# A four-layer vision network on one core: the selective scan is moved in place into two PSUM banks, the rows of C come by DMA, and one bank is shared by the convolutions, heads, tables and offsets

## The reference

```python
# layers 0, 2, 3, on every image
xp = x @ w_in + b_in
h = gelu(batchnorm(depthwise_conv3x3(x)))
offset = (h @ w_off + b_off).reshape(N, H, W, 4, 9, 2)
mask = softmax((h @ w_msk + b_msk).reshape(N, H, W, 4, 9))
y = (bilinear_sample(pad(xp), pixel + tap + offset) * mask).sum(taps) @ w_out + b_out
x = x + gamma1 * layer_norm(y); x = x + gamma2 * layer_norm(gelu(x @ w_fc1 + b_fc1) @ w_fc2 + b_fc2)

# layer 1: 256 inner channels, 16 states, 4 directions k, L = 3136 pixels
xb = silu(depthwise_conv3x3(xx) + conv_b)         # xx, z = split(layer_norm(x) @ in_proj)
dt, B, C = softplus(...), ..., ...                # per direction, from x_proj(xb)
for t in pixels of direction k:
    h = h * exp(dt_t * A) + dt_t * u_t * B_t      # [256 channels, 16 states]
    y_t = (h * C_t).sum(states)
```

## Time and profile before

| | |
|---|---|
| median of three runs | 33311.78 us |
| the profiled execution | 33289.16 us, its span 33287.3 us |
| busy, share of the span | PE 75%, DVE 67%, ACT 36%, POOL 76% |
| granted TensorE clock, mean | 0.82 |
| DMA engines | 56 GB/s, 1,201,869 packets |

### The profile page before, as it was taken

How to read it: one execution, slowest core, us unless ns; L and a number is a source line. 1 busy time by engine, 2 the same in 40 slices (tenths; PEclk the granted TensorE clock), 3 DMA queues, 4 the chain that set the end, 5 groups by cost and what they waited for, 6 DMA issues and landing times.

```text
span 33287.3 us, 293513 instructions
## 1 busy us (share of the span) xinstructions
PE 24914.8 (75%) x101616; PEld 16138.7 (48%) x101616; DVE 22464.4 (67%) x31608; ACT 11949.6 (36%) x20587; POOL 25332.0 (76%) x21604
## 2 busy tenths in 40 slices
PE   6588787878888887888888788787577876555544
PEld 5444454545445554554455445454454545444443
DVE  1289959896988789789968996997149992211211
ACT  1144434444444444444444444443134442010100
POOL 5787868877887787778778787777777877767767
PEclk7698888888888888898889888888688887666666
DMA  2211121212112121211121112111221212222211
GB/s 64 66 52 52 50 64 43 58 48 62 51 50 58 52 57 47 63 51 50 54 58 57 48 53 65 45 55 52 63 69 44 58 49 67 60 62 61 62 55 51
DMA packets 1201869, 1854.06 MB, mean 56 GB/s; under 512 B 391531, under 2 KB 750493, under 8 KB 1200381
## 3 DMA queue, kind: packets, MB, share of 16 engines
q0 software_dynamic: 691200, 1388.65, 15.4%
q1 hardware_dynamic: 509180, 446.64, 4.2%
HBM read 1568.56 MB, written 265.21 MB: 55 GB/s over the span
## 4 chain that ended last, share of the span: by engine, by line
POOL 33%; PE 27%; DVE 23%; issue 14%; ACT 1%; DMA 1%; DVEq 0%; SPq 0%; POOLq 0%; ACTq 0%
POOL d_g L664 33%; DVE l_wk L1197 10%; PE d_p L928 7%; PE l_acc L915 5%; DVE l_wk L1219 4%; DVE l_wk L1187 3%; PE d_pr L1066 2%; PE d_pr L1065 2%; PE d_pr L1077 2%; DVE d_g L1232 2%; PE l_pm L963 2%; PE l_pc L885 1%; PE d_pr L1131 1%; PE l_pm L941 1%; PE l_pc L1041 1%
## 5 line engine op out<-in xcount | busy, mean ns | idle before, releaser
L664 POOL DMA_INDIRECT d_g<-table,d_idx x21600 | 25331.7, 1173 | 7921.9 <-issue 6559.3
L928 PE MATMUL d_p<-d_g,c_ident 128*128 128x128 f32 x43200 | 6879.2, 331 | 4002.6 <-DVE d_g L1232 4001.5
L928 PEld LDWEIGHTS d_p<-d_g,c_ident 128*128 128x128 f32 x43200 | 6639.9, 241 | 4818.7 <-DVE d_g L1232 3783.0
L915 PE MATMUL l_acc<-l_wk,c_ident 128*128 128x448 f32 x14336 | 7276.6, 637 | 0.4 <-DVE l_wk L1219 0.4
L1232 DVE TENSOR_TENSOR d_g<-d_g,d_wt 128x1536 f32<-128x1536 f32 (+1 forms) x1800 | 3151.5, 1751 | 5481.9 <-DMA d_g<-table,d_idx 5480.1
L1197 DVE TENSOR_TENSOR_SCAN l_wk<-l_wk,l_carry 128x448 f32<-128x448 f32 x6144 | 6715.5, 1133 | 0.0
L1187 DVE TENSOR_TENSOR l_wk<-l_wk,l_pb 128x896 f32<-128x896 f32 x3584 | 3864.5, 1078 | 1609.2 <-PE l_pb L885 1603.5
L707 ACT ACTIVATE l_wk<-l_wk,l_a 128x448 f32<-128x448 f32 x7168 | 4361.8, 656 | 16.4 <-DVE l_wk L1261 3.6
L885 PE MATMUL l_pc<-l_spl,c_sel 96*128 96x448 bf16 x3584 | 1402.4, 391 | 3569.2 <-DVE l_wk L1219 3556.7
L915 PEld LDWEIGHTS l_acc<-l_wk,c_ident 128*128 128x128 f32 x14336 | 3135.8, 219 | 1835.5 <-issue 1717.1
L1219 DVE TENSOR_TENSOR l_wk<-l_wk,l_pc 128x896 f32<-128x896 f32 x3584 | 3798.0, 1060 | 9.3 <-PE l_pc L885 8.6
(11 more groups left out here) (169 smaller groups left out, 22973.9 us busy)
## 6 DMA issues: line engine op xcount, KB each, us to landing
d_g<-table,d_idx POOLq DMA_INDIRECT x21600
table<-d_pst SPq DMA_DIRECT2D x600, 256.0 KB, 2.1
hd<-d_hst SPq DMA_DIRECT2D x168, 224.0 KB
d_htc<-hd SPq DMA_DIRECT2D x144, 256.0 KB
d_xin<-mid SPq DMA_DIRECT2D x112, 224.0 KB, 3.0
mid<-d_xo SPq DMA_DIRECT2D x192, 128.0 KB
d_xres<-mid SPq DMA_DIRECT2D x192, 128.0 KB
d_xin<-in_x SPq DMA_DIRECT2D x56, 224.0 KB, 3.0
```

The lines of the kernel that those rows point to most:

```text
L664: e.indirect_dma_start(out=m.g[Q % SLOTS][0:n, j, :], out_offset=None, in_=m.table[k % 2], in_offset=bass.IndirectOffsetOnAxis(ap=m.idx[G ...
L915: ins = e.matmul(m.acc[:, h, 0:448], m.ident[:, :], m.hb[x % 4][:, h, :], start=(n == 0), stop=(n == 15))
L928: ins = e.matmul(m.p0[0:n, t % 2 * 128:t % 2 * 128 + 128], m.ident[0:n, 0:n], m.g[Q % SLOTS][0:n, 4 * p:4 * p + 4, 32 * r:32 * r + 32], st ...
```

## The change

- **Scan.** `hb` is three tiles in place of four and holds only the product with C. The product with B goes to `l_bb`, two PSUM banks (`m.bb`); both scans run in place there, VectorE copies the last column to `carry` itself (not in the last chunk of a direction), and the product with C reads `l_bb` and writes `hb`. A step now runs whole before the next: product with B, two scans, copy, product with C, each but the last waiting for the one before (`hc`, `f_pb`, `sc`).
- **Rows of B and C.** TensorE spreads only B, one step ahead. C's 16 rows of a piece go to DRAM (`cd`) by DMA at head part 1; SyncE then issues for each step one DMA that repeats a row over 128 partitions into one of three tiles `cb` (229 KB each), two steps ahead.
- **Banks.** `l_pc` and `l_pm` are gone. Layer 1's convolution and head share `m.r[1]` with the stages' `ax`, `ac`, `at` and `pr`. The norms and projections between images use the halves `b0`, `b1` of `l_bb`.
- **Order.** An item that fills `m.r[1]` and the one that empties it are now one item of the list, and at most one such item is put in a tick. Convolutions are done in halves of 224 columns, all nine taps in one tick, so the weights are loaded twice as often. `PREP` is one tick shorter (11 ticks in place of 12, if the bank is free). `xin` is one tile in place of two.

The diff, cut to its core:

```diff
@@ vss_ticks
-                out += [(0.5, [("c", i, c, h, part)]) for part in range(4)]
+                out += [(0.8, [("c", i, c, h, part)]) for part in range(2)]
...
-                if j + 2 < 7 and 8 <= q:
-                    tick.append(("c", i, j + 2, (q - 8) // 4, (q - 8) % 4))
+                if j + 2 < 7 and 8 <= q and q % 2 == 1:
+                    tick.append(("c", i, j + 2, (q - 9) // 4, (q - 9) // 2 % 2))
...
-PREP = [0, 2, 1, 0, 1, 1, 1, 1, 1, 1, 1, 1]
+PREP = [0, 2, 0, 0, 1, 1, 1, 1, 1, 1, 1, 1]
@@ Planner.scan_tick
+            self.used = self.used or x[0] == "c" or x[0] == "h" and x[3] in (0, 3, 5)
@@ Planner.stage_tick
-        if self.loads and self.loads[0][1] <= self.fetched + 1 and self.there(*self.loads[0]):
+        if self.loads and self.loads[0][1] <= self.fetched and self.there(*self.loads[0]):
+            self.loads_at = self.tick
...
+        if self.prep and self.prep[0][0][3] == 1:
+            if not self.used and self.tick - self.prep_at >= PREP[1]:
+                for _ in range(3):
+                    self.put(*self.prep.popleft()[0])
+                self.used, self.prep_at = True, self.tick
+        elif self.prep and self.tick - self.prep_at >= self.prep[0][1]:
+            self.put(*self.prep.popleft()[0])
+            self.prep_at = self.tick
+        if self.ahead and not self.used and self.open(self.ahead[0]):
+            use = self.ahead.popleft()
+            for x in use:
+                self.put(*x)
+            self.used = use[0][0] != "al"
...
+        self.used = False
@@ Mem
-        self.wk = [sb(f"l_wk{i}", [128, 2, 448]) for i in range(12)]
+        self.wk = [sb(f"l_wk{i}", [128, 2, 448]) for i in range(11)]
+        self.cb = [sb(f"l_cb{i}", [128, 448]) for i in range(CROWS)]
+        self.bb = ps("l_bb", [128, 2, 512])
+        self.b0, self.b1 = self.bb[:, 0, :], self.bb[:, 1, :]
+        self.cd = [dram(f"cd{i}", (16, 448)) for i in range(2)]
@@ sync_program
+        elif kind == "h" and item[3] == 1:
+            e.wait_ge(s["hd0"], P + 1)
+            if P >= 2:
+                e.wait_ge(s["hc"], 16 * (P - 1))
+            e.dma_start(m.cd[P % 2], m.bcd[16:32, :]).then_inc(s["cdo"], 16)
+        elif kind == "s":
+            for q in (range(CROWS - 1) if sig == -1 else (sig + CROWS - 1,) if sig >= 0 else ()):
...
+                    if S >= CROWS:
+                        e.wait_ge(s["hc"], S - CROWS + 1)
+                    e.dma_start(m.cb[S % CROWS][:, :], m.cd[P % 2][n:n + 1, :].to_broadcast([128, 448])).then_inc(s[f"cb{S % CROWS}"], 16)
@@ scalar_program
-                e.activation(m.carry[:, :, n], m.hb[(S - 1) % 4][:, :, end], ACT.Copy).then_inc(s["ca"], 1)
@@ tensor_program
-            if 0 <= sig < NSTEP:
-                if J.use["C", S]:
-                    e.wait_ge(s["f_pc"], J.use["C", S])
-                spread(S, m.pc, 16).then_inc(s["p_pc"], 1)
...
-                e.wait_ge(s["f_pc"], J.free("C", x))
+                e.wait_ge(s["hc"], x + 1)
...
+            for j in range(9):
+                dy, dx = 4 * part + j // 3, j % 3
+                ins = e.matmul(m.r[1][:, 0:224], m.cdiag[:, 9 * h + j, :],
+                               m.grid[:, h, 8 * c + dy:8 * c + dy + 4, dx:dx + 56], start=(j == 0), stop=(j == 8))
@@ vector_program
-                e.tensor_tensor(m.hb[x % 4][:, :, :], m.dtu[P % 2][:, :, :], bc(m.pb[:, 0:448], 1, 2),
-                                ALU.mult).then_inc(s["f_pb"], 1)
...
+                if S:
+                    e.wait_ge(s["hc"], S)
+                bu = m.bb[:, :, 0:448]
+                e.tensor_tensor(bu, m.dtu[P % 2][:, :, :], bc(m.pb[:, 0:448], 1, 2), ALU.mult).then_inc(s["f_pb"], 1)
+                e.wait_ge(s["dA"], S + 1)
                 e.wait_ge(s["f_pb"], J.free("B", S))
                 for h in range(2):
                     ini = 0.0 if c == (6 if kd >= 2 else 0) else m.carry[:, h, n:n + 1]
-                    ins = e.tensor_tensor_scan(m.hb[S % 4][:, h, way], m.dA[S % 3][:, h, way], m.hb[S % 4][:, h, way], ini,
-                                               ALU.mult, ALU.add)
+                    ins = e.tensor_tensor_scan(bu[:, h, way], m.dA[S % 3][:, h, way], bu[:, h, way], ini, ALU.mult, ALU.add)
                 ins.then_inc(s["sc"], 1)
+                e.wait_ge(s["sc"], S + 1)
+                if c != (0 if kd >= 2 else 6):
+                    end = 0 if kd >= 2 else 447
+                    e.tensor_copy(m.carry[:, :, n], bu[:, :, end])
+                e.wait_ge(s[f"cb{S % CROWS}"], 16 * (S // CROWS + 1))
+                if S >= 3:
+                    e.wait_ge(s["accd"], S - 2)
+                e.tensor_tensor(m.hb[S % 3][:, :, :], bu, bc(m.cb[S % CROWS][:, :], 1, 2), ALU.mult).then_inc(s["hc"], 1)
...
-                e.wait_ge(s["p_pc"], J.full("C", x))
-                e.wait_ge(s["ca"], x + 1)
-                e.tensor_tensor(m.hb[x % 4][:, :, :], m.hb[x % 4][:, :, :], bc(m.pc[:, 0:448], 1, 2),
-                                ALU.mult).then_inc(s["f_pc"], 1)
```

More of the change, by code:

```diff
@@ L239, in run @@
         self.start_ahead(0)
-        self.drain(lambda: not self.ahead and not self.bank)
+        self.drain(lambda: not self.ahead)
         self.start_prep(0, 0)
-        self.drain(lambda: not self.prep and not self.bank)
+        self.drain(lambda: not self.prep)
         self.chain += [(("lg", 0), 0), (("lg2", 0), 1)]
@@ L251, in run @@
                 if t % 4 == 0:
-                    self.drain(lambda: not self.prep and not (self.bank and self.bank[0][0][0] == "pr"))
+                    self.drain(lambda: not self.prep)
                     if g + 1 < len(GROUPS):
@@ L619, in sync_program @@
             q = 7 * i + c
[L620 removed]
+            e.wait_ge(s["f_b1"], J.free("pt", q))
             if i:
@@ L880, in tensor_program @@
     e.wait_ge(s["cst"], 1)
-    def spread(S, bank, row):
-        P, n = divmod(S, 16)
-        return e.matmul(bank[:, 0:448], m.sel[:, row + n:row + n + 1].to_broadcast([96, 128]), m.spl[P % 2][:, :],
-                        start=True, stop=True)
     for item in J.plan:
```

443 lines of the change are left out of this document (198 added, 245 removed).

## The result

The changed kernel takes **34,278 us** (median of 4 runs, 34,229 to 34,290; 33,288 for the kernel before beside it): **2.9% slower**, ratio 1.0294, interval 1.0276 to 1.0312. I had forecast 32,500 us, 2.4% faster. The profiled execution has a span of 34,279 us, against 33,287.

What follows compares the result with a forecast made beforehand. VectorE with its waits for TensorE bounded the scan stretches, GpSimd the rest. Scans 19,555 + 1,190 + 220 + 750 + 300 = 22,015, rest 10,467, together 32,482: forecast 32,500 us, range 31,500 to 33,650.

Steps and rivals of the forecast that it cites:

- POOL is freed: Beside scans, GpSimd's need falls to about 18,630 us, 16.8 us a third; by itself this buys almost nothing.
- VectorE's step: In scan stretches, new dependences cost 860 and 80 us and the carry copy 246: +1,190 us in sum.
- PSUM operands at 0: VectorE's products and scans with PSUM operands cost nothing extra; bounds -215 to +645 us.
- TensorE: In scan stretches, bunched bank fills against about 9 us of room leave waits for B of 750 us, before 1,603.
- The other waits: VectorE's other idle time in the scan stretches, some 350 us before, was put at 300 us.
- my chief rival: TensorE and ScalarE hand over the one shared bank, holding B back 1.5 us a fill: 34,050 us, chance 0.17.
- The pace: Planner's pace falls from 3.14 to 2.92, 85 more thirds beside scans: -1,314 us outside the stretches, +220 us within.
- Small terms: C's row loads free; +25 us between images, +60 for the shared bank without scans, -120 for GpSimd's earlier start.
- The 120 us that I took off: GpSimd enters the two stretches free of scans some 60 us further ahead: -120 us.
- a step that grows by more than 0.4 us: Sign against the forecast: VectorE's scan step, 4.08 us before, lengthens by more than 0.4 us.
- the rival with 34,050: Shared bank's hand-over between TensorE and ScalarE makes waits 2,300 us, not 750; chance 0.17, left outside the range.
- terms 2 and 4: Scan stretches: VectorE's longer step, +1,190 us, and its waits for TensorE's spread of B, 750 us.

Runs made afterwards that it cites:

- run 302: Not a follow-up run: the words say that 302 us of the 1,797 us missed lie in the rest of the run, outside the scan stretches.
- a_sbuf: Changed kernel with B's product and both scans written in an SBUF tile instead of the two PSUM banks: 34,300 us.
- a_order: Changed kernel with VectorE's two waits ahead of a step's first scan in the other order: 34,152 us.
- a_fill: Changed kernel with TensorE's spread of B moved from behind a third's twelve accumulations to behind the first four: 33,886 us.
- a_sep: Changed kernel with B's product and scans in SBUF, and layer 1's convolutions and heads on the bank this frees: 34,294 us.
- a_prep: Changed kernel with VectorE's two operations that empty the bank of offsets moved to the start of the next tick: 34,118 us.
- a_nocb: Changed kernel with C's rows loaded for the first three steps only and reused in every step: 34,299 us.
- a_short: Changed kernel with one tap of nine in all depthwise convolutions, every wait and emptying kept: 33,569 us.

## Why the prediction was wrong, step by step

The trace's 34,279 us less my sum of 32,482 is 1,797 us. The stretches of scans have 1,495 of it, the rest of the run 302.

1. *POOL is freed*: right. The gathers' mean is 1,030 ns (forecast 1,060). That this is worth nothing by itself is right too (a_sbuf).
2. *VectorE's step*: right mechanism, size too small. I had two dependences at 0.12 us, a copy at 0.08, a fifth of a third dependence, 1,190 us in all. Measured are 0.44 us, 1,580 us. One dependence cost 0.185, because its wait is an instruction of its own (a_order). My 20,965 us for VectorE in the stretches had the dependences in it. To compare, its busy time of 20,789 takes the 376 us of gaps in front of the first scans and 160 us of gaps under 0.06 us: 21,325, **+360 us**.
3. *PSUM operands at 0*: right (a_sbuf, 22 us apart).
4. *TensorE*: **this step failed.** I gave it 9 us of room and put the wait for B at 750; it is 1,391: **+641 us**. I counted the room from the moment at which VectorE frees B's bank. But TensorE works in order, and in a tick with a third it can't begin before VectorE's product L1214, the last of a tick. From there it has one step, 4.5 us, for the accumulations and the spread, not 9; moving the spread forward took off 471 us (a_fill). The end of the 3,557 us wait for C did let TensorE come earlier: where VectorE waits for a spread that has a third ahead of it, the accumulations start 3.0 us after the product's end in the kernel before and 0.15 us in the changed one (medians of 578 of 782 and 576 of 754 waits). But it can't come earlier than the product, and I had the passes too cheap: a third's take 4.13 us, 1.39 a tick, where I put 1.0. At 2.9 us, the time at the upper clock, passes and spread would fit into the step; of the 574 waits right behind a third's passes 467, 892 of 1,144 us, follow passes in which the clock was below 0.95. How much of the +641 the clock accounts for stays open. And 275 of the 574, 911 us, are of another kind than the one shown above: TensorE had no idle time ahead of the third, so it was late already. The other waits, which I put at 300 us, are 794 (345 norms, 334 offsets, 115 others): **+494**. The sharing of the bank by layer 1 and the stages, the core of my chief rival, has no part in either (a_sep); the shared tick has 92 us of the offsets' wait (a_prep).
5. *The pace*: right. The planner found 2.948 (forecast 2.92); 1,202 thirds run beside scans (1,212). The ten thirds are 150 us of the **+302** outside.
6. *Small terms*: C's rows free, right (a_nocb). The shared bank outside the scans was put at +60; ahead of the first scan alone it is 152 us, 92 more (a_short takes 115 of the 152 away). The 120 us that I took off for GpSimd's further start into the two free stretches didn't come: these shrank by 1,176 us, 75 thirds at 15.5 are 1,162. Between the other images it is 22 us less where I had 25 more. With the ten thirds this is the 302.

My own list of signs had "a step that grows by more than 0.4 us" as one that would tell against the forecast. The range ended at 33,650, because I let the rival with 34,050 stay outside, and because terms 2 and 4 both came out high and I had added no case in which they do so together.

What stays open: how much the lower clock costs in the wait for B; of this wait 645 us remain without bunched passes and with the spread moved, and of the offsets' wait 242. TensorE's lateness there has several kinds of items in front of the spread, and I didn't take them apart.

## What to carry to other kernels

Room on an in-order engine is counted from the last thing in its order that it can't start early, not from the moment at which its output buffer comes free; look for a short idle of that engine just ahead of a late product. Price its passes with the clock that it has there: here 24 passes took 2.9 or 5.4 us, and more of them took long when the idle time stood in one piece ahead of them. Making operations in place turns overlap between neighbours into dependences: price it by the step's start-to-start times, and look for waits that stand as instructions of their own. And an engine that is freed is worth something only with the knob that gives it more work: try the old kernel with that knob too, for here it alone gave 1.7%.

## What the runs showed of the hardware

- VectorE neighbours overlap by 0.08 to 0.09 us when independent; a dependence puts 0.034 us between them, with its wait as an own instruction 0.104. Two halves of 128x448 (0.53 us from start to start each) are shorter than one 128x896 product with a dependence behind it (1.19).
- An instruction's two waits: the one written first went into the instruction, the other stood alone (a_order against the changed kernel). The order in which waits are written was worth 126 us.
- A scan with a PSUM operand and result costs 1,141 ns against 1,139 in SBUF, but gathers beside it are no longer stretched: 944 ns where one meets nothing but a scan (1,477 in the kernel before), and 1,030 for 1,121 in the mean of all.
- 820 MB of loads with one row repeated over 128 partitions, 24 MB in each 1,000 us, cost the kernel no time (a_nocb).
- 24 fp32 passes of TensorE of 128 columns took 2.9 us at a granted clock of 1.0 and 5.4 at 0.5. Behind more than 2 us of idle time the clock was 0.60 in the mean (518 thirds), else 0.84.
